# Reordered ends of a Mamba-style block with a butterfly feed-forward net: mixing steps, weight loads and the bias add moved to other places in their queues

## The reference, cut to what matters

```python
# first half: state-space block on the layer norm of x, added to x
xz = layernorm(x) @ in_proj_w.T                      # 256 -> 2*512
x_inner, z = split(xz)
x_conv = silu(causal_depthwise_conv(x_inner, 4 taps) + conv_b)
x_dbl = x_conv @ x_proj_w.T                          # 512 -> 1 + 16 + 16
delta, B, C = softplus(x_dbl[..., 0]), x_dbl[..., 1:17], x_dbl[..., 17:]
h = h * exp(delta * A) + x_t * (delta * B)           # scan over the tokens, state 512 x 16
y = (h @ C + x_conv * D) * silu(z)
x1 = x + y @ out_proj_w.T
# second half: feed-forward net on the layer norm of x1, added to x1
h = butterfly(layernorm(x1) @ W_exp + b_exp, up_weights)    # 10 stages on 1024 features
h = gelu(h + up_bias)
out = x1 + butterfly(h, down_weights) @ W_con + b_con + down_bias
```

## Time and profile before

| | us |
|---|---|
| median of 3 runs | 561.27 |
| lowest, highest | 560.69, 564.58 |
| the profiled execution | 566.98 |
| its span, first to last instruction | 564.9 |

### The profile page before, as it was taken

How to read it: one execution, slowest core, us unless ns; L and a number is a source line. 1 busy time by engine, 2 the same in 40 slices (tenths; PEclk the granted TensorE clock), 3 DMA queues, 4 the chain that set the end, 5 groups by cost and what they waited for, 6 DMA issues and landing times.

```text
span 564.9 us, 8225 instructions
## 1 busy us (share of the span) xinstructions
PE 521.1 (92%) x3012; PEld 427.4 (76%) x3012; DVE 414.1 (73%) x892; ACT 307.9 (55%) x537; POOL 91.4 (16%) x88
## 2 busy tenths in 40 slices
PE   4986899799999999999999999999999999769987
PEld 3764676576788888887888789778888887658876
DVE  4858999657994899489966997599848784645532
ACT  3766883656128751785259623972287418621342
POOL 4040200320011300150013201320113001210110
PEclk9987988979999999999999999999999999889999
DMA  9543311200021101210112001200111011100011
GB/s 231 112 27 5 77 38 38 62 16 1 2 75 39 39 2 37 75 41 0 39 38 77 1 16 62 70 8 2 37 44 35 2 38 40 38 1 0 1 38 37
DMA packets 42635, 21.75 MB, mean 39 GB/s; under 512 B 26435, under 2 KB 41027, under 8 KB 42596
## 3 DMA queue, kind: packets, MB, share of 16 engines
q1 hardware_dynamic: 39956, 17.57, 13.0%
q10 hardware_dynamic: 2640, 3.67, 2.3%
HBM read 16.78 MB, written 4.46 MB: 38 GB/s over the span
## 4 chain that ended last, share of the span: by engine, by line
PE 50%; DVE 19%; ACT 11%; issue 10%; SPq 6%; POOL 2%; DMA 1%; ACTq 0%; DVEq 0%; POOLq 0%
PE acc L872 11%; PE wide L861 10%; PE wide L850 9%; PE wide L710 8%; DVE xc L1490 5%; SPq L424 5%; PE wide L824 4%; DVE state L1595 3%; PE wide L835 2%; ACT xc L1160 2%; PE small L700 2%; DVE diag_sum L1613 2%; DVE diag L1609 2%; DVE hid_low L1507 1%; ACT L1160 1%
## 5 line engine op out<-in xcount | busy, mean ns | idle before, releaser
L1120 ACT ACTIVATE hid_f<-wide,bias_up 128x512 f32<-128x512 f32 x64 | 43.9, 686 | 169.7 <-PE wide L861 166.4
L1490 DVE SCALAR_TENSOR_TENSOR xc<-xi,taps,xc 128x512 f32<-128x512 f32 x96 | 83.7, 877 | 4.6 <-ACT xc L1151 2.3
L872 PE MATMUL acc<-w_down_high,hid_high 128*128 128x256 f32 x256 | 73.0, 285 | 3.1 <-DVE hid_low L1507 3.0
L872 PE MATMUL acc<-w_down_high,hid_low 128*128 128x256 f32 x256 | 72.0, 281 | 0.0
L872 PE MATMUL acc<-w_down_low,hid_high 128*128 128x256 f32 x256 | 72.0, 281 | 0.0
L1507 DVE TENSOR_TENSOR hid_low<-hid_f,hid_high 128x512 fp32r<-128x512 f32 x64 | 45.5, 714 | 30.4 <-ACT hid_high L1233 30.0
L530 POOL TENSOR_TENSOR rstd<-var_eps,minus_half 128x4 f32<-128x4 f32 x16 | 19.7, 1233 | 286.9 <-DVE var_eps L1396 286.9
L710 PE MATMUL wide<-xnT_ln1T_high,w_in_high 128*128 128x512 f32 x128 | 57.3, 448 | 6.1 <-ACT xc L1151 3.2
L861 PE MATMUL wide<-xnT_ln2T_high,w_up_high 128*128 128x512 f32 x128 | 55.1, 430 | 4.9 <-DVE xnT_ln2T_low L1501 4.9
L850 PE MATMUL wide<-w_out,xc 128*128 128x256 f32 x256 | 58.5, 388 | 0.9 <-DVE xc L1657 0.5
L850 PEld LDWEIGHTS wide<-w_out,xc 128*128 128x128 f32 x256 | 49.2, 195 | 8.2 <-issue 1.5
(11 more groups left out here) (193 smaller groups left out, 1048.1 us busy)
## 6 DMA issues: line engine op xcount, KB each, us to landing
x_res<-in_L_attn_x_dram SPq DMA_DIRECT2D x9, 512.0 KB, 3.5
c_near<-c_of_tokens SPq DMA_DIRECT2D x8, 512.0 KB
x_ln<-in_L_attn_x_dram SPq DMA_DIRECT2D x7, 512.0 KB, 3.6
out_dram<-x1b_xn SPq DMA_DIRECT2D x7, 512.0 KB, 2.9
xc<-in_L_attn_in_proj_w_dram ACTq DMA_DIRECT2D x2, 512.0 KB, 6.7
xc<-in_L_ffn_W_exp_dram ACTq DMA_DIRECT2D x1, 1024.0 KB, 11.9
x1b_xn<-in_L_ffn_W_con_dram ACTq DMA_DIRECT2D x1, 1024.0 KB, 15.3
raw_out<-n_L_attn_out_proj_w_dram ACTq DMA_DIRECT2D x1, 512.0 KB, 7.7
```

The source lines that it names most:

```text
L872: last = pe.matmul(acc[:, c, :], hid[h][:, j % HRING, c * P:(c + 1) * P], w_down[w][:, j, 0:DM], start=j == 0 and c % 2 == 0 and n == 0, s ...
L1120: ins = act.activation(out_ap, in_ap, how.pop("func"), **how)
L1490: ins = dve.scalar_tensor_tensor(xc[u % BATCH][:, e, :], xi[:, e, tap:tap + TILE], taps[:, e, tap:tap + 1], xc[u % BATCH][:, e, :], ALU.mu ...
```

## The change

- **Loads.** The 14 DMAs of DOWN's low weights are issued by ACT, behind W_con and ahead of its first copy, in place of SP. On SP `spread_c(0)` stands ahead of `load_for_norm(2)`.
- **Phase 0.** The transposes, high parts and low parts of unit 1's input come earlier on PE, ACT and DVE. On DVE `add_blocks(DOWN, 2)` moves from before `weigh_b` to behind the gates and the paths of DOWN, and `add_blocks(UP, 1)` moves out of phase 0.
- **Phase 1.** `add_blocks(UP, 1)` follows the softplus; on ACT `scale_blocks(UP, 2)` moves behind the high parts of ln2T and `prepare(15)` one place ahead.
- **GpSimd.** `residual_with_bias(u - 1)` moves from the start of phase u to behind `b_with_c(u)` and the rstd of u + 2, with a wait for all four gates of u.
- **The last unit.** PE takes up 3 before y and one further up or down between the parts of y and the output projection, and transposes unit 7's input for the net before down 6 and 7. DVE makes m_mat before the state and unit 7's low parts before `final`. ACT does gelu 2 behind the exponentials. The order list follows.

The work itself, its shapes and its counts stay the same.

```diff
--- before.py
+++ after.py
@@ -20,6 +20,7 @@
 from contextlib import ExitStack
+from itertools import islice
 
...
@@ -72,11 +73,13 @@
     WIDE_ORDER += uses(("xp", [0]), of=phase) + uses(("in", range(8)), of=phase + 1)
-    between = phase >= HALVES_FROM
-    WIDE_ORDER += uses(("up", range(3)), of=phase - 1) + uses(("y", range(2)), of=phase)
-    WIDE_ORDER += uses(("up", [3] if between else []), of=phase - 1) + uses(("y", range(2, CB)), of=phase)
-    WIDE_ORDER += uses(("up", [4] if between else [3, 4]), of=phase - 1) + uses(("out", range(2)), of=phase)
-    WIDE_ORDER += uses(("up", range(5, HB)), of=phase - 1)
+    first, between, then = (3, 0, 2) if phase < HALVES_FROM else (3, 1, 1) if phase + 1 < UNITS else (4, 1, 1)
+    ups = iter(range(HB))
+    some_ups = lambda many: uses(("up", list(islice(ups, many))), of=phase - 1)
+    WIDE_ORDER += some_ups(first) + uses(("y", range(2)), of=phase)
+    WIDE_ORDER += some_ups(between) + uses(("y", range(2, CB)), of=phase)
+    WIDE_ORDER += some_ups(then) + uses(("out", range(2)), of=phase)
+    WIDE_ORDER += some_ups(HB)
     SMALL_ORDER += uses(("xtok", range(GR)), ("xdtok", [0]), of=phase)
...
@@ -454,7 +457,6 @@
                                  weights[LOW + s].rearrange("(q p) o i -> p q (o i)", p=P)).then_inc(s_loaded, 16)
-            load_low(sp, DOWN, down_weights)
             def load_for_norm(u):
...
@@ -483,8 +485,8 @@
 
+            spread_c(0)
             load_for_norm(2)
-            spread_c(0)
             load_for_residual(0)
...
@@ -600,14 +602,15 @@
             for u in range(UNITS):
-                if u:
-                    residual_with_bias(u - 1)
                 weigh_gaps(u)
...
                     rstd_of(u + 2, 0, var1, rstd1)
+                if u:
+                    wait(pool, gated, u, CB)
+                    residual_with_bias(u - 1)
                 rstd_of(u, 1, var2, rstd2)
...
@@ -901,9 +904,9 @@
                 prepare(4)
+                transposes(1, "ln1T", x_ln, norm1)
                 prepare(5)
                 prepare(6)
-                transposes(1, "ln1T", x_ln, norm1)
                 pe.wait_ge(masks_made, 2)
...
@@ -964,6 +967,26 @@
                 off_diagonal(u)
+                up(p, 3)
+
+            def last_outputs(u):
+
+                p = u - 1
+                ssm_output_halves(u, 0)
+                down(p, 2)
+                up(p, 4)
+                ssm_output_halves(u, 1)
+                down(p, 3)
+                up(p, 5)
+                down(p, 4)
+                out_projection(u, 0)
+                out_projection(u, 1)
+                up(p, 6)
+                down(p, 5)
+                up(p, 7)
+                transposes(u, "ln2T", xn2, norm2)
+                down(p, 6)
+                down(p, 7)
 
...
@@ -988,6 +1011,9 @@
                     down(p, 0)
+                if v == UNITS:
+                    last_outputs(u)
+                    return
                 if u < HALVES_FROM:
...
@@ -995,8 +1021,7 @@
                     up(p, 3)
-                    if v < UNITS:
-                        down(p, 1)
+                    down(p, 1)
                     ssm_output_halves(u, 1)
...
@@ -1025,7 +1050,6 @@
             def last_ffn(u):
-                transposes(u, "ln2T", xn2, norm2)
                 for j in range(HB):
...
@@ -1065,6 +1089,7 @@
             act.dma_start(raw_con, W_con.rearrange("(g p) d -> p g d", p=P)).then_inc(w_loaded["con"], 16)
+            load_low(act, DOWN, down_weights)
 
...
@@ -1240,10 +1265,10 @@
                 prepare(4)
+                high_parts(1, "ln1T")
                 prepare(5)
+                place_halo(1)
                 scale_blocks(DOWN, 0)
-                place_halo(1)
-                high_parts(1, "ln1T")
                 exp_sums(0)
...
@@ -1283,17 +1308,17 @@
                 exp_abs(u)
-                beside("abs")
                 if v == UNITS:
                     load_gelu_table()
-                    for j in range(3):
-                        gelu(p, j)
+                    gelu(p, 0)
+                    gelu(p, 1)
                     load_exp_table(2)
...
                     high_parts(p, "ln2T")
+                    beside("ln2T")
                 if v < UNITS:
...
@@ -1304,9 +1329,9 @@
                     copy_z(v, 5)
+                beside("z 5")
                 take_c_start(u)
                 exp_diagonal(u)
-                beside("diagonal")
                 if v < UNITS:
...
@@ -1319,7 +1344,7 @@
                     beside("gelu 1")
-                    gelu(p, 2)
+                gelu(p, 2)
                 gelu(p, 3)
...
@@ -1332,9 +1357,9 @@
             def weights_of_ffn(place):
-                if place == "abs":
+                if place == "ln2T":
                     scale_blocks(UP, 2)
-                elif place == "diagonal":
+                elif place == "z 5":
                     prepare(15)
...
@@ -1699,15 +1724,14 @@
                 softplus(0)
+                low_parts(1, "ln1T")
                 multiply_short_paths(UP)
                 sum_biases()
-                low_parts(1, "ln1T")
                 take_sums(0)
...
                 weigh(0)
-                add_blocks(DOWN, 2)
                 weigh_b(0)
...
@@ -1723,8 +1747,8 @@
                 multiply_whole_paths(DOWN)
+                add_blocks(DOWN, 2)
                 add_blocks(UP, 0)
-                add_blocks(UP, 1)
                 low_parts(2, "ln1T")
...
@@ -1756,17 +1780,14 @@
                 v, r, p = u + 1, u + 2, u - 1
-                if v < UNITS:
-                    convolve(v, 0)
+                convolve(v, 0)
                 diagonal_times_c(u)
...
                 advance_state(u)
-                if v < UNITS:
-                    low_hidden(p, 0)
+                low_hidden(p, 0)
                 assemble(u)
-                if v < UNITS:
-                    convolve(v, 1)
-                    low_hidden(p, 1)
+                convolve(v, 1)
+                low_hidden(p, 1)
                 if r < UNITS:
...
@@ -1775,8 +1796,19 @@
                 low_hidden(p, 3)
-                if v < UNITS:
-                    convolve(v, 2)
+                convolve(v, 2)
+
+            def to_last_outputs(u):
+
+                p = u - 1
+                diagonal_times_c(u)
+                sum_diagonal(u)
+                assemble(u)
+                low_hidden(p, 2)
+                advance_state(u)
+                gates_of_halves(u, 0)
+                low_hidden(p, 3)
+                gates_of_halves(u, 1)
 
...
@@ -1785,6 +1817,7 @@
                 softplus(u)
+                beside("step")
                 if v < UNITS:
...
@@ -1798,8 +1831,10 @@
                     to_first_outputs(u, beside)
+                elif v < UNITS:
+                    to_outputs_in_halves(u)
                 else:
-                    to_outputs_in_halves(u)
+                    to_last_outputs(u)
                 low_hidden(p, 4)
...
@@ -1812,10 +1847,14 @@
                 low_hidden(p, 7)
+                if v == UNITS:
+                    low_parts(u, "ln2T")
                 final(p)
...
             def weights_of_ffn(place):
-                if place == "softplus":
+                if place == "step":
+                    add_blocks(UP, 1)
+                elif place == "softplus":
                     add_blocks(UP, 2)
...
@@ -1841,7 +1880,6 @@
                 phase(u)
-            low_parts(UNITS - 1, "ln2T")
             low_hidden(UNITS - 1, *range(HB))
```

## The result

| | before | after |
|---|---|---|
| median, us | 562.13 (4 runs) | 586.06 (4 runs) |
| lowest to highest | 560.69 to 564.58 | 585.46 to 587.42 |
| profiled execution | 566.98 | 587.42 |
| its span | 564.9 | 585.2 |

A forecast was written before the change was run, and what follows sets the result against it. TensorE was taken to bound the middle (58.77 of 59.40 us busy), with looser ends. Terms +27.3 - 7.5 + 0.5 - 8 = +12.3 on 561.3 gave 573.6 us (568 to 579 for the forecast itself); range 557 to 587.

The forecast's parts named there:

- The lot on ACT: Start: ACT issuing the contraction's 14 low transfers makes unit 0 27.3 us late; bounds 6.2 to 36.
- rival 3: Start: the two lots slow each other, 36 us of delay, 582 us in all; chance 0.15.
- rival 1: Start: issues on ACT are cheap, 6.2 us or little more, 552.5 us in all; chance 0.15.
- The head: Unit 0's exponential to phase 2's start: reordering gives -7.5 us, bounds -4 and -10; 134.4 us for 141.9.
- The terms 4.1, 2.0 and 1.5: Gains in us: TensorE up to x_projection(1), phase 1's normalising no longer held, TensorE's wait for ACT's UP 2.
- C's earlier round trip: Phase 0: C spread earlier, so GpSimd's c_near product falls before the 12 taps; 2.0 us gained.
- The 3.57 us wait for the high weights: Phase 0: ACT's wait goes; weigh_b comes 4.1 us earlier, 3.57 of the wait and 0.5 of order.
- "free" for UP 1: Phase 1: UP 1's 3.25 us fit where VectorE waits 3.29 us for ACT, if ACT comes no earlier.
- The middle: Units 1 to 6: GpSimd's add behind the gates costs +0.5 us over five units, bounds -0.5 and +2.5.
- The last unit: Last x_projection to the end: reordering gives -8 us, bounds -5 and -10; 83.5 us for 91.5.
- new waits: Last unit: down 4 waits 1.0 us for a split behind the last gates, down 5 2.0 behind the statistics.
- The carry-over: Whole kernel: the difference from the profiled execution, 566.98 us, should carry over to the median, 561.27.

## Why the prediction was right or wrong, point by point

**The lot on ACT: the step that failed, by its size.** I took 27.3 us "as on SP at the same time of the run", and it is 36.9 at unit 0 (37.6 at ACT). The mechanism was right (ACT issues in order and does nothing else, and unit 0 waits for all of it), and so were the signs given for it: the table load behind 14 issues, one of over 5 us, no wait for the high weights. What was wrong is to price the lot as if it were alone. The run with one lot at a time gives 23.87, near what I took and below it; side by side both lots stretch until their sum, about 41 us, is worked off. That is rival 3 (36 us, 582), which I gave 0.15. Rows of before would have allowed more weight: 27.32 + 16.30 = 43.6 us of issuing was there to be seen, and nothing said that two issuers would each get a full share. The DMA share of 0.14 doesn't clear the DMA engines. It is a mean over 16 engines, and it isn't bounded by 1: in the run with the rows split on ACT the same four microseconds show 2.04, which can only come of packet times that overlap.

```profile
20.00:24.00 4.00, 0.00 (x0) 0.00 (x0) 0.00 (x0) 0.00 (x0) 0.00 (x0) 1.00 2.04 70
```

Rival 3's reason, the few engines that both second stages go to, isn't borne out as the main cause: spreading the rows of the stages with 2 and 4 partitions took 2.5 of 37.6 us off ACT's lot. Averaged over the pieces, 7,168 to a lot, the price is 2.3 ns each in 16.30 us and 2.8 ns of the common 40.8 us, the big loads' part included.

**The rule of the Trainium skill** ("DMA: Bandwidth & Descriptors", Issuing engines are not separate DMA queues), that issuing is usually short beside the transfer, would have led to rival 1 (552.5). No run shows when these transfers landed, so the two times can't be set side by side. But a lot in 8-byte pieces held its issuer for 16.3 us or more in every run, so issuing wasn't cheap here in the sense of rival 1; the same 14 transfers in 254 pieces come nearest to it (9.79 us, 559.26 in all).

**The head.** Forecast -7.5 from the step's exponential of unit 0 to phase 2: 134.4 us; measured 204.50 - 71.26 = 133.24. The terms 4.1, 2.0 and 1.5 make 7.6, not 7.5, which changes nothing. The parts fell otherwise. Phase 0 gave 6.7 for 4.1, phase 1 gave 2.0 for 3.5. I gave 2.0 us to C's earlier round trip, for the port that its product held across the taps. In fact with the taps earlier, C's round trip behind the lot is the next thing late and costs a wait of 5.84 us on VectorE; freeing it is 4.8 of the 6.7, and all the rest of the new order 1.8 (phase 0 is 71.50, 69.66 and 64.83 us in the kernel before, with the lot ahead of C, and behind it). The 3.57 us wait for the high weights was worth nothing in this order: with a wait of 2.92 still there on SP, the stretch from exponential to x_projection(1) takes 57.71 us, and without it 57.68. The 12 taps at 9.03 and the normalising at 1.39 came as forecast.

Phase 1's 2.0 us are luck in part, and "free" for UP 1 was not right. TensorE's wait of 3.2 us for ACT is gone, but VectorE is busy for 63.92 us of the phase, where the old order has 57.61 to 59.37, and TensorE now waits for it instead:

```profile
PE small L762 <- DVE xnT_ln2T_low L1526: 2.5, 1, 2.5
```

The rows of the whole phase, in the changed kernel and in the version with the state first (busy time of PE, PEld, DVE, ACT, POOL, then the granted clock), are:

```profile
128.94:204.50 75.56, 69.01 (x388) 55.29 (x387) 63.92 (x142) 41.66 (x79) 11.98 (x8) 0.98 0.10 29
...
98.21:172.66 74.45, 66.80 (x387) 53.87 (x386) 57.61 (x131) 38.98 (x71) 11.44 (x8) 1.00 0.10 29
```

With the new order and the add behind the gates, phase 1 takes 75.5 to 75.6 us in each of nine traces, whether the granted clock falls in it or not. With the old one it takes 77.6 to 78.3 in three traces, in which the clock falls, and 74.45 in the one at full clock (below). So the new order gains 2 to 3 us where the clock falls in the old one and loses 1.1 where it doesn't.

**The middle.** Forecast +0.5, measured -0.34 for five units. The add does what was said, 2.1 us more on three taps, and VectorE has the room.

**The last unit.** Forecast -8, measured -7.55. The terms that I gave make 7.2 (7 for m_mat, 1.4 for up 3 and 1.8 for the last wait, less 3.0 of new waits), so 0.8 of the 8 had no source. y's first product comes 6.98 us earlier, behind the last x_projection, for the 7 forecast. m_mat's wait went from 5.3 to 0.84, the new waits are 0.76 for the 1.0 and 2.12 for the 2.0 forecast. With the state first it is 3.87 us longer, for the 3.05 I took. What I hadn't: behind down 5's wait, its 12 products take 2.80 us for 1.71 in the run with the lot back on SP, at a granted clock of 0.66 for 1.00 in the 4 us around them, which is 1.1 of the 1.5 us between this tail and the 82.42 there. So one and the same code has a tail of 82.4 or of 84.0 us, and against before's 91.51 that is 9.1 or 7.55.

**The carry-over.** I added the difference to the median. Before's profiled execution stands 4.85 us above its median (566.98, 562.13), after's only 1.36 (587.42, 586.06); so 3.5 of the 23.9 us are no segment of either trace, but the place of the two profiled executions among the others. In the three later groups of runs the kernel before has medians of 565.84, 564.47 and 565.4, so the 562.13 beside the changed kernel is the low one, and 23.9 us may be 2 to 4 too many; the changed kernel wasn't run beside those groups. With the lot at 36.9 the sum of my own terms is 36.9 - 7.5 + 0.5 - 8 = 21.9, for the 20.3 of the spans.

## What to carry to other kernels

Price a lot of transfers by the pieces that it is cut into, not by its bytes or by the DMA share, and put a lot of thousands of pieces on an engine with no computing behind it; the packets per queue on a run's page show them. A single issue of the lot can't be priced so. Two lots that each stall their issuer should be added up, not laid side by side, until a run shows that they don't share what limits them. When a step is brought forward, look for what else of its inputs is now late (here C's round trip, 4.8 of the 6.7 us of phase 0 by the traces), and see which engine takes the work that moved: UP 1 turned a wait for ACT into one for VectorE. Before a difference of 2 us in one segment is explained, look at the segment in every trace with the same code.

## What the runs showed of the hardware

- Two engines issuing small-piece transfers at once take as long together as in turn: 40.8 us for 41.2 (and for 43.6 in the kernel before). Which common part it is stays open. The DMA share (a sum of packets' times, see above) is 0.33 from 20 to 24 us in the changed kernel and 0.14 before:

```profile
20.00:24.00 4.00, 0.00 (x0) 0.00 (x0) 0.00 (x0) 0.00 (x0) 0.00 (x0) 1.00 0.33 7
```

- Phase 1 took 77.56, 78.21 and 74.45 us in the kernel before, with the last unit's edits alone, and with the state first, where its code is the same (and 78.27 with only the lot moved to ACT). In the first three TensorE waits 3.2 us for ACT some 13 to 15 us into this phase, at 112.24, 111.55 and 111.69. In two windows of 6 us around it the granted clock, the column behind POOL's, is down in one execution and full in another (the first fence is of the last unit's edits alone, the second of the version with the state first):

```profile
108.41:114.41 6.00, 2.86 (x9) 2.36 (x10) 2.55 (x12) 5.97 (x14) 2.10 (x2) 0.79 0.32 87
114.41:120.41 6.00, 6.00 (x28) 5.38 (x29) 5.78 (x18) 3.23 (x8) 0.18 (x1) 0.64 0.01 3
```
```profile
110.21:116.21 6.00, 4.52 (x27) 3.98 (x28) 2.90 (x7) 5.94 (x13) 1.73 (x2) 1.00 0.32 87
116.21:122.21 6.00, 5.17 (x33) 4.16 (x32) 4.72 (x14) 3.09 (x7) 1.83 (x2) 1.00 0.00 0
```

  So two single profiles of one code may differ by 3 to 4 us in this phase. Why the clock falls in one and not in the other isn't known.
- Whether GpSimd's add holds VectorE hangs on the landing of a store: where the add began 0.13 us behind the step's first instruction, that one took 0.17 us, not the 2.17 of the earlier trace rows.
